# Rotary attention: rotated query parts from halves of the query's own product, in place of a second product with permuted weights

## The reference, cut to what matters

```
def _pos_emb(k_len):
    pos = jnp.arange(k_len - 1, -1, -1)
    inv = 1.0 / 10000.0 ** (jnp.arange(0, HEAD_DIM, 2) / HEAD_DIM)
    s = pos[:, None] * inv[None, :]
    return jnp.concatenate([jnp.sin(s), jnp.cos(s)], axis=-1)
...
q = sh(xn @ Wq.T + bq); k = sh(xn @ Wk.T + bk); v = sh(xn @ Wv.T + bv)
scores = einsum('bhqd,bhkd->bhqk', q, k)
rel = einsum('bhqd,ld->bhql', q + u[None, :, None, :], _pos_emb(S))
scores = (scores + _rel_shift(rel, S, S)) * HEAD_DIM ** (-0.5)
# causal mask, softmax, @ v, @ Wo.T + bo
```

## Time and profile before

| | us |
|---|---|
| median of 3 runs | 6759.97 (6751.65 to 6768.34) |
| the profiled execution | 6756.28 |
| its span in the trace | 6754.2 |
| PE busy | 5795.9 (86%) |
| DVE busy | 4329.9 (64%) |
| ACT busy | 2805.1 (42%) |
| POOL busy | 1939.8 (29%) |

### The profile page before, as it was taken

The page is one execution under the profiler, slowest core; times in us unless marked ns, Lnnn a source line. Parts: engine busy times, 40 slices in busy tenths (PEclk is TensorE's granted clock), DMA queues, the critical chain, the costliest instruction groups (busy, mean ns, idle before and its releaser), DMA issues. The chain is left out here.

```text
span 6754.2 us, 122147 instructions
## 1 busy us (share of the span) xinstructions
PE 5795.9 (86%) x38509; PEld 3594.7 (53%) x38509; DVE 4329.9 (64%) x9722; ACT 2805.1 (42%) x4568; POOL 1939.8 (29%) x2617
## 2 busy tenths in 40 slices
PE   8996999999993998889987998799888889845567
PEld 5773444444442776467745775477545556523454
DVE  6874666666655775367736774477545466669965
ACT  4552222222221554345543554355444455412244
POOL 5440000000003553255414552355310022333312
PEclk9998999999996999899998999899988899867789
DMA  4332222233223553155504551355300000000002
GB/s 129 104 101 91 96 96 95 96 96 97 95 93 82 144 149 94 31 143 146 138 4 131 149 150 33 88 145 149 80 4 0 3 0 0 4 3 0 0 2 57
DMA packets 526309, 526.84 MB, mean 78 GB/s; under 512 B 55698, under 2 KB 436705, under 8 KB 503780
## 3 DMA queue, kind: packets, MB, share of 16 engines
q1 hardware_dynamic: 526004, 523.15, 27.6%
HBM read 337.88 MB, written 185.07 MB: 77 GB/s over the span
## 5 line engine op out<-in xcount | busy, mean ns | idle before, releaser
L362 DVE TENSOR_REDUCE a_mx<-a_unit 128x2 f32<-128x512 f32 (+1 forms) x1920 | 1294.3, 684 | 574.8 <-PE a_unit L538 562.6
L452 ACT ACTIVATE a_prob<-a_slot 128x1536 f32<-128x1536 f32 x640 | 929.0, 1452 | 740.9 <-PE a_slot L561 448.5
L536 PE MATMUL a_unit<-a_sk,a_sq 96*128 96x256 bf16 (+3 forms) x5120 | 756.3, 251 | 75.2 <-DMA a_sk<-a_kscratch 54.1
L1148 ACT ACTIVATE f_silu<-f_pG 128x512 f32<-128x512 f32 x528 | 315.1, 598 | 939.3 <-PE f_pG L1221 939.1
L1094 DVE TENSOR_TENSOR f_gated<-f_spread,f_silu 128x512 f32<-128x512 f32 x512 | 354.3, 692 | 402.8 <-ACT f_silu L1148 358.3
L538 PE MATMUL a_unit<-a_maskq,identb 128*128 128x256 bf16 (+1 forms) x1920 | 606.3, 316 | 0.0
L1200 PE MATMUL f_pO<-f_hidden,f_wd 128*128 128x512 f32 x1056 | 546.3, 599 | 17.0 <-DVE f_hidden L1096 16.3
L536 PEld LDWEIGHTS a_unit<-a_sk,a_sq 96*128 96x128 bf16 (+1 forms) x5120 | 385.3, 99 | 312.1 <-issue 124.8
L1221 PE MATMUL f_pG<-f_xnT,f_wg 128*128 128x512 f32 x1056 | 541.5, 594 | 0.0
L1225 PE MATMUL f_pU<-f_xnT,f_wu 128*128 128x512 f32 x1056 | 540.9, 594 | 0.0
L60 POOL TENSOR_SCALAR f_veps<-f_moments 128x4 f32<-128x4 f32 (+1 forms) x112 | 25.4, 227 | 1731.3 <-DVE f_moments L1002 1271.4
(11 more groups left out here) (394 smaller groups left out, 11507.0 us busy)
## 6 DMA issues: line engine op xcount, KB each, us to landing
f_spread<-f_scratch SPq DMA_DIRECT2D x1024, 128.0 KB, 2.9
a_sq<-a_qscratch SPq DMA_DIRECT2D x128, 768.0 KB, 5.7
a_sk<-a_kscratch SPq DMA_DIRECT2D x160, 384.0 KB, 6.6
a_qscratch<-a_parts SPq DMA_DIRECT2D x288, 192.0 KB, 2.2
a_qscratch<-a_parts SPq DMA_DIRECT2D x288, 128.0 KB, 2.2
a_kscratch<-a_parts SPq DMA_DIRECT2D x160, 192.0 KB, 2.2
a_kscratch<-a_parts SPq DMA_DIRECT2D x160, 128.0 KB, 2.1
a_qscratch<-a_parts SPq DMA_DIRECT2D x288, 64.0 KB, 1.8
```

The lines of the kernel that those rows point to most:

```text
L362: v.tensor_reduce(dst, src, op=ALU.max, axis=AX.X, negate=True).then_inc(red_done, 1)
L452: act.activation(prob[gr % 2][:, :], slot[:, :], ACT.Exp, scale=SCALE).then_inc(exp_done, 1)
L536: pe.matmul(bank[:, at * wide:(at + 1) * wide], q, sk[b][0:KM, gr * GH + h, 0:wide], start=(at == 0), stop=False)
L1148: act.activation(silu[c % 2][:, :], pG[c % 2][:, :], ACT.Silu).then_inc(silu_done, 1)
```

## The change

The second product (line 653) with its weights `u12`, their load and its semaphore u_pe are taken out. DVE instead reads the q product of line 631, which is still in `ring[1]`: the A half (partitions 0 to 63) gives both halves of u1, and the B half (partitions 64 to 127) both halves of u2, in four scalar_tensor_tensor over 64 partitions. Those with an output half other than their input half write across partitions. DVE now waits for qk_taken in place of u_pe. The table `turn` is laid out by input partition instead of by output partition.

```
--- before.py
+++ after.py
@@ -170,7 +170,7 @@
     READS = 2
     WRITES = 9 if rel else 6
     UNITS = 3 * GROUPS
-    W_QK = 16 * (5 if rel else 2)
+    W_QK = 16 * (4 if rel else 2)
     W_OUT = 16 * 3
     SCALE = float(HD) ** -0.5
     with ExitStack() as stack_:
@@ -194,7 +194,7 @@
         ctxp = k.sb("ctxp", [P, BLK])
         rec = k.sb("rec", [P, QT * HEADS]); cn = k.sb("cn", [P, QT, D]); cT = k.sb("cT", [P, SEQ])
         if rel:
-            lnw = k.sb("lnw", [P, 2]); u12 = k.sb("u12", [P, 2 * D])
+            lnw = k.sb("lnw", [P, 2])
             b12 = k.sb("b12", [P, 4]); b12s = k.sb("b12s", [P, 2])
             turn = kept.turn; u1 = k.sb("u1", [P, SEQ]); u2 = k.sb("u2", [P, SEQ])
         else:
@@ -219,7 +219,7 @@
         mrow_out = [k.sem(f"mrow_out{b}") for b in range(4)]
         mrow_in = [k.sem(f"mrow_in{b}") for b in range(4)]
         if rel:
-            u_pe, u_taken, u_added, b12_done = k.sem("u_pe u_taken u_added b12_done")
+            u_taken, u_added, b12_done = k.sem("u_taken u_added b12_done")
         else:
             guard_done, osb_done = k.sem("guard_done osb_done")
 
@@ -234,7 +234,7 @@
                     arriving.first(sp)
                 loads = [(wq[:, :], w["wq"]), (bqk[:, :], w["bqk"])]
                 if rel:
-                    loads = [(lnw[:, :], w["lnw"])] + loads + [(b12[:, :], w["b12"]), (u12[:, :], w["u12"])]
+                    loads = [(lnw[:, :], w["lnw"])] + loads + [(b12[:, :], w["b12"])]
                 for dst, src in loads:
                     sp.dma_start(dst, src if layer is None else src[layer]).then_inc(w_qk, 16)
                 for dst, src in ((bo[:, :], w["bo"]), (wo[:, :], w["wo"]), (bv[:, :], w["bv"])):
@@ -412,13 +412,16 @@
                         v.wait_ge(kept.loaded, kept.loads)
                         v.wait_ge(b12_done, 1)
                     if rel and is_seq(n + 4):
-                        v.wait_ge(u_pe, n + 5)
+                        v.wait_ge(qk_taken, n + 5)
                         if is_seq(n + 3):
                             v.wait_ge(u_added, n + 4)
-                        v.scalar_tensor_tensor(out=u1[:, :], in0=ring[1][:, 0:SEQ], scalar=b12s[:, 0:1],
-                                               in1=turn[:, 0, :], op0=ALU.add, op1=ALU.mult)
-                        v.scalar_tensor_tensor(out=u2[:, :], in0=ring[1][:, SEQ:2 * SEQ], scalar=b12s[:, 1:2],
-                                               in1=turn[:, 1, :], op0=ALU.add, op1=ALU.mult).then_inc(u_taken, 1)
+                        for c, u in ((0, u1), (1, u2)):
+                            low = slice(c * D // 2, (c + 1) * D // 2)
+                            for o in range(2):
+                                ins = v.scalar_tensor_tensor(out=u[o * D // 2:(o + 1) * D // 2, :], in0=ring[1][low, 0:SEQ],
+                                                             scalar=b12s[low, c:c + 1], in1=turn[low, o, :],
+                                                             op0=ALU.add, op1=ALU.mult)
+                        ins.then_inc(u_taken, 1)
                     units(8, 12)
                     if is_seq(n - 1):
                         dst = rows(store, (n - 1) * QT, QT)
@@ -647,12 +650,6 @@
                     maxima(6)
                     values(n, j % 2, 1)
                     maxima(7)
-                    if rel and is_seq(n + 4):
-                        pe.wait_ge(qk_taken, n + 5)
-                        for c in range(2):
-                            ins = pe.matmul(ring[1][:, c * SEQ:(c + 1) * SEQ], u12[:, c * D:(c + 1) * D], xnT[j % 4][:, :],
-                                            start=True, stop=True)
-                        ins.then_inc(u_pe, 1)
                     maxima(8)
                     if is_seq(n - 1):
                         pe.wait_ge(c_taken, n)
@@ -2570,7 +2567,8 @@
     ang = np.arange(SEQ)[None, :] * inv[:, None]
     sin, cos = np.sin(ang), np.cos(ang)
     turn = np.stack([np.concatenate([sin, -cos]), np.concatenate([cos, sin])], 1)
-    c["turn"] = np.repeat(turn, HEADS, 0).astype(np.float32)
+    turn = np.repeat(turn, HEADS, 0).astype(np.float32)
+    c["turn"] = turn.reshape(2, D // 2, 2, SEQ).transpose(2, 1, 0, 3).reshape(D, 2, SEQ)
     kt = np.concatenate([cos, sin]).astype(np.float32)
     parts = []
     for _ in range(3):
@@ -2601,7 +2599,6 @@
         wq=np.concatenate([T(wq)[:, :, BY_R], T(wk)[:, :, BY_R], T(wv)], 2), wo=T(wo)[:, PAIRED],
         bqk=np.stack([bq[:, BY_R], bk[:, BY_R]], 2), bv=bv[:, PAIRED, None], bo=bo[:, None, :],
         lnw=np.stack([lnw, lnb], 2),
-        u12=np.concatenate([T(wq)[:, :, TURN_A], T(wq)[:, :, TURN_B]], 2),
         b12=np.stack([bq[:, TURN_A], bq[:, TURN_B], uf[:, TURN_A], uf[:, TURN_B]], 2))
 
 
```

More of the change, by code:

```diff
@@ L649, in step @@
                     maxima(7)
[L650 to L655, removed]
                     maxima(8)
```

## The result

The changed kernel takes 6858.5 us in the median (4 runs, 6838.6 to 6864.6) against 6755.8 (4 runs); the ratio is 1.0146, 95% interval 1.0119 to 1.0173, so 1.5% or some 99 us slower. The forecast was 0.8% slower, 6815 us, with a range to 6838. The direction held; of the 99 us the forecast had 55, a little over half, and the measured time lies 20 us above its range.

What follows compares the result with a forecast made beforehand. A loop through DVE, POOL, SP, DMA and PE was taken as the bound: 15 x 1.01 us a layer less fill gains, net 13.8, 55 in all, on 6756.3 gives 6811, plus 3.7 for the median: 6815 us, range 6766 to 6838.

Steps and rivals of the forecast that it cites:

- PE was not the bound: Rel attention: PE's order sets no pace; the rival that it does, 0.86 us a step won, 6650 us, had 4%.
- two-step loop: Rel attention: DVE, POOL, SP, DMA queue and PE up to unit 7, 32.50 us over two steps, sets the pace.
- middle links: POOL's adds and split, 6.53 us, then SP's writes and loads until scores(0), 13.49 us.
- 64 partitions cost what 128 do: Each new STT on DVE takes 0.48 us as now; the rival of half price, 6733 us, had 5%.
- slow end: The four STTs on DVE start 0.55 us apart, each waiting for the one before; the overlap rival, 0.40 us, had 24%.
- first link: From the end of unit 7's reduction to the last STT's end on DVE: 1.04 us, to grow by 1.01.
- The loop's share: Rel layers: 15 traverses of 1.01 us more, less what the fill gives back: 13.8 us a layer, 55 in all.
- What PE wins it spends in a longer wait at the next scores(0).: PE's 0.86 us a step from the removed product lie outside the loop and only lengthen its wait.
- the clock as a rival at 3%: PE idles more, its granted clock falls to 0.93, its 11.44 us grow 7%: 52 us on top, 6867; chance 3%.
- Each link starts on the end of the one before it, without slack: The four links of the loop through DVE, POOL, SP, DMA and PE join without gaps, 16.25 us a step.

Runs made afterwards that it cites:

- e3: The changed kernel with two STTs of 128x256 on the q product in place of the four of 64x256 (values wrong): 6768.5 us, ratio 1.0012.
- e5: The changed kernel with four STTs of 128x256 that never change halves (values wrong): 6848.5 us, ratio 1.0150.
- e9: e1 plus four useless PE matmuls ahead of the wait for the maxima rows in each rel step: 6809.4 us, ratio 1.0077.
- e6n: The kernel before, second product kept, with four STTs of 128x256 for two and the maxima parts of e1: 6806.8 us, ratio 1.0077.
- e10: The changed kernel plus four useless PE matmuls ahead of the wait for the maxima rows in each rel step: 6821.8 us, ratio 1.0098.
- e1: The changed kernel with both maxima parts made by DVE reductions over one element, low part left out: 6855.2 us, ratio 1.0137.
- e4: The changed kernel with the four STTs moved ahead of the reductions of units 6 and 7: 6723.2 us, ratio 0.9942.
- e14: The kernel before plus four useless PE matmuls ahead of scores(0) in every rel step: 6787.2 us, ratio 1.0046.

## Why the prediction was wrong

Right, by its steps: PE was not the bound, and the product that went was worth nothing (e3); the STTs sit on a two-step loop through POOL, SP and the DMAs, whose middle links didn't move; 64 partitions cost what 128 do (e5); each STT that turns to other halves starts behind the end of the one before it. The pitch of the slow end was 0.05 us too long, so the first link grew by 0.85 and not 1.01 us. The rule of the Trainium skill ("VectorE: DVE Perf Modes", section "Two Vector instructions with no wait between them") is borne out here: with a change of halves the starts lie 0.50 us apart, each 0.01 us behind the end of the one before; without, 0.39 apart, each 0.08 ahead of that end. (The Trainium skill compares every input of an instruction and not the first alone; here all inputs of one STT start at the same partition.) The loop's share, 55 us in the sum, was measured near 52 us, in e9 and e6n (0.77%, 0.60 to 0.93; 41 to 63 us). That the two lie so close is in part luck: with the measured pitch the same sum gives (15 x 0.85 - 1.08 - 0.5) x 4 = 45 us.

The step that failed is the one that priced PE's added idle time at nothing: "What PE wins it spends in a longer wait at the next scores(0)." That wait has a price. Behind waits of 1.1 to 3.4 us PE's granted clock fell to the lower level (1.2 GHz) 27 times in the steady parts, against 8 before, and 25 more of 128 v products ran slow. Between the change and e10, which takes these away, stand 1.0146 and 1.0098, some 33 us; between e1 and e9 0.60%, 41 us, 1.6 us for each slow step. Since the loop spans two steps it fixes only their sum, and the wait can fall on one of them whole: in e5 the steps alternate between 15.8 and some 18.6 us (starts of the STTs, 2306 to 2425), so a mean wait of 1 us a step is met as 2 us in every second. The prediction had the clock as a rival at 3%, wrongly seen as a lower clock all through and weighed by a mean busy share (85% busy at 1.00); in these traces the low stretches stand behind single waits.

The second miss is in "Each link starts on the end of the one before it, without slack": true of the rows before, but it named the only loop looked for. The cast of line 387, held by POOL until line 342 ends, made a second one some 0.1 us behind, which takes the full 0.85 us. Its share by time is small, some 14 us between e9 and e10, and e1 against the change shows none. That the cast ends with line 342 is shown by the rows; what the hold costs by itself rests on e9 against e10 alone, where the times don't overlap and the intervals of the ratios do. So the 99 us are 52 (e9), 14 (e10 over e9) and 33 (the change over e10). These three add up by how they are taken, one ratio after the other, and are no check of each other; taken in another order the shares differ (e1 over e9 gives the clock 41).

## What to carry to other kernels

Before pricing the idle time that a change gives an engine at nothing, look at how long the single waits become: in this kernel a PE wait of some 2 us cost 1.3 to 1.6 us more behind it where the clock fell. When a loop over engines sets the pace, list every other loop within the price of the change, above all one that spans fewer steps, since it charges the same delay more often. And when a new instruction reads something that is ready earlier than what it replaces, move it up: the same four STTs are 1.5% slower at one place and 0.6% faster at another.

## What the runs showed of the hardware

A DVE cast of 128x32 from f32 to bf16, SBUF to SBUF, takes 0.17 us alone and up to 1.65 us beside POOL's tensor_tensor of 128x768. In the change 70 of the 128 casts of line 387 in the rel layers took over 0.3 us, and each ended 0.03 to 0.04 us behind the end of an instruction of POOL, line 342 in 38 of them and the cast of line 341 in 30. A cast that started ahead of POOL's instruction took 0.17 us beside it. A tensor_reduce over an axis of one element, which does the same work, took 0.17 to 0.19 us all 128 times, 88 of them beside lines 341 and 342 (e1). PE's clock fell to its lower level behind single waits of 1.1 to 3.4 us in the steady part of the change, in some steps and not in others: waits of 1.76, 2.09 and 2.49 us passed without it in the first layer. In e4 waits of 1.2 us in every step brought no low stretch at all. Four matmuls whose results nobody reads made one kernel 0.6% faster (e1 to e9) and another 0.5% slower (e14).
